# Copying the queries of a batch's first group in two halves, in a cross attention kernel on one Trainium2 core

## The chip, the core and the metric

The kernel runs on one core of a Trainium2 chip. The metric is the device time of one execution in microseconds (us), as the median of some runs. Matrix products run on TensorE (PE in the profile; its weight loads are a row of their own, PEld). Elementwise work runs on VectorE (DVE), ScalarE (ACT) and GpSimd (POOL). SyncE (SP) issues most of the DMA transfers. The engines run side by side and hand work over by semaphores: an instruction raises one when it is finished, and another engine's instruction waits until it has reached a value.

## The reference, cut to what matters

`x` is 32 batches of 512 tokens of width 640, and `ctx` is 32 batches of 77 text tokens of width 1024. There are 20 heads of width 32. The reference also has three other attention branches (object, others, ip), whose contexts are empty slices here, so that only the text branch counts:

```python
q = _heads(hidden_states @ to_q_w)                 # 32 x 20 x 512 x 32
k, v = _heads(ehs_txt @ to_k_w), _heads(ehs_txt @ to_v_w)   # 32 x 20 x 77 x 32
s = jnp.einsum('bhqd,bhkd->bhqk', q, k) * scale
p = jax.nn.softmax(s, axis=-1)
out = _merge(jnp.einsum('bhqk,bhkd->bhqd', p, v))
out = out @ to_out_w + to_out_b + hidden_states
```

## The kernel before, in words

There are two phases. `project_context` splits the weights into a high and a low part and computes keys and values of all batches into DRAM; it takes about the first 316 us. `attend` does the rest, and the change is there alone.

`attend` goes through 32 batches, and in each through 5 groups of 4 heads (`CC = 5` groups of 128 columns, `QT = 4` tiles of 128 queries). Every engine has an order written out by hand, one string for each group (lines 66 to 81), and all engines run their strings independently, held together by semaphores alone. A letter is an operation of that group's step:

- TensorE: `S` are the scores of this group (`scores`, L755: 4 tiles x 4 heads, 16 calls and 32 matmul instructions). `Q0` to `Q4` project the queries of the *next* group into the PSUM bank `q_bank` (`project_q`, L743, 15 matmuls). `P` and `O` are output projections of earlier batches (15 matmuls each), and `V` is the product of the probabilities with the values, two groups back (`sum_values`, L770, 8 instructions).
- VectorE: `M` is the maximum over the keys (`maxima`, L636), `R0` to `R3` the reciprocals of the sums of a tile, `T0` to `T3` the transposes of its probabilities, `Q` the copy of `q_bank` to `q_t` in SBUF (`copy_q`, L657, one instruction of 512 columns), `W` a correction of the head outputs, `X` and `Y` prepare x of the next batch, and `O`, `P`, `Z` finish outputs.
- ScalarE: `S0` to `S3` are the exponentials of the four tiles (`exps`), `V` a copy of the head outputs. GpSimd: `N0` to `N3` multiply the probabilities with the reciprocals.

The strings of a batch's last group are what the change touches:

```
TensorE  g=4:  S O2 Q0 Q1 Q2 Q3 Q4 V      then g=0 of the next batch:  S Q0 ...
VectorE  g=4:  M X2 X3 X4 W R0 R1 T0 O2 R2 T1 Q R3 T2 T3    then:  M W Z0 ...
VectorE  g=0:  M W Z0 R0 Q R1 T0 Z1 R2 T1 R3 T2 Z2 T3 P3
```

In the groups 0 to 3 TensorE has an output projection between the last `Q` and the next `S` (but for the start of the run); in group 4 it has only `V`. The scores wait for the keys of the batch (only in group 0), for the exponentials of the group before (`exp_done`, they free the PSUM bank) and for the copy of the queries (`q_ready`), then raise `scores_clear`, for which no engine waits. The profile shows waits that don't fit into an instruction as EVENT_SEMAPHORE instructions of TensorE's sequencer: one at L761 in each group, and a further one at L760 in the first group of a batch, where there are three waits.

Of the kernel before, what the change touches and what calls it, by code (L numbers as in the profile page):

```python
# [28 lines left out]
CC = C // P  # L29
KC = CA // P  # L30
QT = S // P
# [59 lines left out]
def cross_attention(nc, x, ctx, wq, wk, wv, wo, bias, out):  # L91
    k_scratch = nc.dram_tensor("k_scratch", (C, TOK), F32, kind="Internal").ap()
    v_scratch = nc.dram_tensor("v_scratch", (TOK, C), F32, kind="Internal").ap()
    p_scratch = nc.dram_tensor("p_scratch", (2, KB, P, HG * P), F32, kind="Internal").ap()
    with ExitStack() as stack:
        def sbuf(name, shape, dtype=F32):
            return stack.enter_context(nc.sbuf_tensor(name, shape, dtype))


        kept = {  # L100
            "x_raw": sbuf("x_raw", [P, 2, S // SQ, CQ]),
            "wq": sbuf("wq_split", [P, 2, CC, C], F32R),
            "wo": sbuf("wo_split", [P, 2, CC, C], F32R),
        }
        x_loaded = stack.enter_context(nc.semaphore("x_loaded"))
        x_v = x.rearrange("b (n q) (i c) -> b i q n c", q=SQ, i=P // SQ)
        out_v = out.rearrange("b (n q) (i c) -> b i q n c", q=SQ, i=P // SQ)
        project_context(nc, ctx, wq, wk, wv, wo, kept, k_scratch, v_scratch, x_v, x_loaded)
        attend(nc, x_v, bias, out_v, kept, k_scratch, v_scratch, p_scratch, x_loaded)
# [305 lines left out]
def attend(nc, x_v, bias, out_v, kept, k_scratch, v_scratch, p_scratch, x_loaded):  # L415

    with ExitStack() as stack:
        def sbuf(name, shape, dtype=F32):
            return stack.enter_context(nc.sbuf_tensor(name, shape, dtype))

        def sem(name):
            return stack.enter_context(nc.semaphore(name))
# [8 lines left out]
        q_t = [sbuf(f"q_t{i}", [P, S]) for i in range(2)]  # L431
# [12 lines left out]
        q_bank, pv_bank, fill_bank = bank[0], bank[1], bank[2:4]  # L444
# [4 lines left out]
        scores_clear, s_done, max_ready, exp_done = sem("scores_clear"), sem("s_done"), sem("max_ready"), sem("exp_done")  # L449
# [1 line left out]
        probs_zero, probs_turned, pv_done = sem("probs_zero"), sem("probs_turned"), sem("pv_done")  # L451
        probs_written = [sem(f"probs_written{i}") for i in range(2)]
        probs_read = [sem(f"probs_read{i}") for i in range(2)]
        q_done, q_ready = sem("q_done"), sem("q_ready")
        ot_high, ot_ready = sem("ot_high"), sem("ot_ready")
        xt_turned, xt_high, xt_ready = sem("xt_turned"), sem("xt_high"), sem("xt_ready")
        out_done, out_added, out_turned, out_stored = (sem("out_done"), sem("out_added"), sem("out_turned"),
# [6 lines left out]
        def tiles_of(columns):  # L464

            return columns.rearrange("p (t i q) -> p t i q", t=QT, q=SQ)

        def rows_of(columns):

            return columns.rearrange("p (i t q) -> p t i q", t=QT, q=SQ)  # L470
# [164 lines left out]
        def _(dve):  # L635
# [21 lines left out]
            def copy_q(n, slot):  # L657
                dve.wait_ge(q_done, n + 1)
                if not (isinstance(n, int) and n < 2):
                    dve.wait_ge(s_done, n - 1)  # L660
                nc.vector.tensor_copy(tiles_of(q_t[slot][:, :]), rows_of(q_bank[:, :])).then_inc(q_ready, 1)  # L661

            def ot_low_part(b, g, parity):
                dve.wait_ge(ot_high, CC * b + g + 1)
# [33 lines left out]
            for c in range(CC):  # L698
                xt_low_part(0, c)
            copy_q(0, 0)  # L700

            def body(b, parity, age, last):
# [37 lines left out]
        def _(pe):  # L740
# [14 lines left out]
            def scores(b, g, slot, parity):  # L755
                if g == 0:
                    pe.wait_ge(k_loaded[parity], DMA // 2 * (b - parity) + DMA)
                if not (isinstance(b, int) and CC * b + g == 0):
                    pe.wait_ge(exp_done, TILES * b + QT * g)
                pe.wait_ge(q_ready, CC * b + g + 1)  # L760
                pe.sem_inc(scores_clear, 1)  # L761
                for t in range(QT):
                    for h in range(HG):
                        rows = slice(h * HD, (h + 1) * HD)
                        last = nc.tensor.matmul(s_bank[:, h, t * N_TXT:(t + 1) * N_TXT],  # L765
                                                q_t[slot][rows, t * P:(t + 1) * P], k_sb[parity][rows, g, :],
                                                start=True, stop=True)
                last.then_inc(s_done, 1)
# [28 lines left out]
            def body(b, parity, age, last):  # L797
                for g, slot, kind, k in steps(TENSOR, b, parity, age, last):
                    if kind == "S":
                        scores(b, g, slot, parity)  # L800
                    elif kind == "Q":
                        project_q(*after(b, g), k)
                    elif kind == "V":
                        sum_values(*before(b, g, parity, 2)[:2], slot)
                    elif kind == "O":
                        project_out(b - 1, k, 1 - parity)
                    elif kind == "P":
                        project_out(b - 2, k, parity)
# [28 lines left out]
```

## Time and profile before

| | |
|---|---|
| time, median of 3 runs | 1820.34 us (1820.07 to 1821.33) |
| the profiled execution: its own time | 1821.04 us |
| its span, first to last instruction | 1819.2 us |
| mean granted TensorE clock | 0.987 |
| PE busy | 1756.4 us, 97% |
| PEld busy | 1364.8 us, 75% |
| DVE busy | 1282.9 us, 71% |
| ACT busy | 1052.6 us, 58% |
| POOL busy | 496.5 us, 27% |

A busy PE is a matmul in flight; matmuls overlap, and their ends are modelled. A row of the timeline is a run of instructions of one line: start, length, engine, line, operation, what is written from what, shapes, count, and in brackets the idle time of the engine before it with what ended it.

### The profile page before, as it was taken

How to read it: one execution, taken by the hardware profiler on the slowest of the kernel's cores; microseconds unless marked ns; L12 is line 12 of the kernel's file. 1: busy time of each engine (PE TensorE's matmuls, PEld its weight loads, DVE VectorE, ACT ScalarE, POOL GpSimd, SP SyncE). 2: the span in 40 equal slices, each digit the busy share in tenths (PEclk: the TensorE clock that was granted, in tenths of full speed). 3: DMA queues.
4: the chain of work that ended last, by engine and by line, in shares of the span. 5: the costliest groups of instructions: out<-in, count | busy, mean ns of one | idle time of the engine just before them, and what ended most of it. 6: DMA issues, size and time to landing. Idle time of an engine off the chain costs nothing.

```text
span 1819.2 us, 38127 instructions
## 1 busy us (share of the span) xinstructions
PE 1756.4 (97%) x13360; PEld 1364.8 (75%) x13360; DVE 1282.9 (71%) x2506; ACT 1052.6 (58%) x5597; POOL 496.5 (27%) x735
## 2 busy tenths in 40 slices
PE   7999996799999999999999999999999999999996
PEld 7999995567777777777777777777777777777764
DVE  5321201678888888888888888888888888888873
ACT  4321211666666666666666666666666666666660
POOL 1111110333333333333333333333333333333330
PEclk9999998899999999999999999999999999999998
DMA  9543112587888888888888888888888888888863
GB/s 229 152 121 92 63 47 58 142 204 214 224 220 223 222 222 224 226 219 221 225 227 219 223 223 223 230 215 222 223 224 229 217 224 223 223 224 224 220 185 103
DMA packets 311599, 357.00 MB, mean 196 GB/s; under 512 B 40240, under 2 KB 194592, under 8 KB 311408
## 3 DMA queue, kind: packets, MB, share of 16 engines
q1 hardware_dynamic: 241648, 301.30, 61.0%
q10 hardware_dynamic: 65472, 40.64, 10.4%
q0 software_dynamic: 4288, 12.62, 2.0%
q8 instruction: 106, 1.74, 0.4%
q14 instruction: 85, 0.70, 0.1%
HBM read 174.10 MB, written 180.39 MB: 195 GB/s over the span
## 4 chain that ended last, share of the span: by engine, by line
PE 78%; DVE 2%; ACT 1%; DMA 1%; issue 1%; POOL 0%; SPq 0%; ACTq 0%; DVEq 0%
PE p_bank L750 31%; PE p_bank L789 29%; PE p_scores L765 9%; PE p_bank L777 8%; ACT probs L597 1%; DVE negmax L638 0%; DMA p_scratch<-turned 0%; DMA out<-out_blocks 0%; DVE turned L654 0%; POOL probs L574 0%; DMA probs_t<-p_scratch 0%; DVE x_t L676 0%; DVE x_raw L671 0%; DVE out_blocks L692 0%; SPq L518 0%
## 5 line engine op out<-in xcount | busy, mean ns | idle before, releaser
L597 ACT ACTIVATE probs<-p_scores,negmax 128x77 f32<-128x77 f32 x2560 | 788.7, 361 | 325.9 <-DVE negmax L638 325.9
L574 POOL TENSOR_TENSOR probs<-probs,rsum 128x308 f32<-128x308 f32 x640 | 447.4, 701 | 1021.1 <-DVE rsum L644 1021.0
L597 ACT ACTIVATION_READ_ACCUMULATOR probs<-p_scores,negmax 128x1 f32 x2560 | 619.5, 242 | 0.0
L750 PE MATMUL p_bank<-x_t,wq_split 128*128 128x512 f32 x2400 | 596.4, 401 | 16.0 <-DVE x_t L676 16.0
L789 PE MATMUL p_bank<-o_t,wo_split 128*128 128x512 f32 x2400 | 574.9, 391 | 0.4 <-DVE x_turned L685 0.4
L750 PEld LDWEIGHTS p_bank<-x_t,wq_split 128*128 128x128 f32 x2400 | 446.8, 190 | 116.3 <-DVE x_t L676 17.2
L789 PEld LDWEIGHTS p_bank<-o_t,wo_split 128*128 128x128 f32 x2400 | 448.7, 188 | 98.0 <-issue 2.5
L654 DVE STREAM_TRANSPOSE turned<-probs 128x384 f32<-128x384 f32 x640 | 352.4, 551 | 39.9 <-POOL probs L574 39.8
L765 PEld LDWEIGHTS p_scores<-k_sb,q_t 32*128 32x128 f32 x5120 | 159.8, 187 | 152.8 <-issue 152.8
L638 DVE TENSOR_REDUCE negmax<-p_scores 128x16 f32<-128x1232 f32 x160 | 230.2, 1438 | 24.0 <-PE p_scores L765 23.8
L604 ACT ACTIVATE o_t<-p_bank 128x512 fp32r<-128x512 f32 x160 | 98.5, 616 | 177.3 <-PE p_bank L777 177.3
L765 PE MATMUL p_scores<-k_sb,q_t 32*128 32x77 f32 x5120 | 182.5, 279 | 18.6 <-ACT probs L597 11.6
L644 DVE RECIPROCAL rsum<-sums 128x4 f32<-128x4 f32 x640 | 107.5, 168 | 125.7 <-ACT probs L597 121.2
L777 PE MATMUL p_bank<-probs_t,v_sb 77*32 77x512 f32 x1280 | 171.3, 607 | 8.6 <-DMA probs_t<-p_scratch 6.3
L661 DVE COPY q_t<-p_bank 128x512 f32<-128x512 f32 x160 | 109.4, 684 | 81.4 <-PE p_bank L750 81.4
L377 PE MATMUL p_bank<-ctx_t,wk_split 128*128 128x256 f32 (+1 forms) x1200 | 147.2, 285 | 9.9 <-DVE wk_split L315 9.6
L377 PEld LDWEIGHTS p_bank<-ctx_t,wk_split 128*128 128x128 f32 x1200 | 146.2, 195 | 10.2 <-DVE wk_split L315 9.6
L397 PE MATMUL p_bank<-wv_split,ctx_t 128*128 128x320 f32 (+1 forms) x960 | 142.2, 309 | 0.0
L397 PEld LDWEIGHTS p_bank<-wv_split,ctx_t 128*128 128x128 f32 (+1 forms) x960 | 139.0, 184 | 1.7
L333 DVE TENSOR_TENSOR ctx_t<-ctx_turned,ctx_t 128x512 fp32r<-128x512 f32 (+1 forms) x40 | 26.7, 668 | 149.1 <-ACT ctx_t L264 148.9
L665 DVE TENSOR_TENSOR o_t<-p_bank,o_t 128x512 fp32r<-128x512 f32 x160 | 108.8, 680 | 0.0
L280 ACT ACTIVATE kv_out<-p_bank 128x320 f32<-128x320 f32 (+1 forms) x40 | 17.5, 437 | 113.0 <-PE p_bank L397 108.0
(30 smaller groups left out, 706.7 us busy)
## 6 DMA issues: line engine op xcount, KB each, us to landing
p_scratch<-turned SPq DMA_DIRECT2D x160, 768.0 KB, 5.9
probs_t<-p_scratch SPq DMA_DIRECT2D x320, 256.0 KB
out<-out_blocks SPq DMA_DIRECT2D x128, 320.0 KB, 5.5
x_raw<-in_x ACTq DMA_DIRECT2D x124, 320.0 KB, 4.4
probs_t<-p_scratch SPq DMA_DIRECT2D x160, 104.0 KB
ctx_raw<-in_ctx SPq DMA_DIRECT2D x32, 256.0 KB, 8.6
k_sb<-k_scratch SPq DMA_DIRECT2D x32, 192.5 KB, 5.1
v_sb<-v_scratch SPq DMA_DIRECT2D x160, 38.5 KB
```

Source lines behind the costliest of these rows:

```text
L377: last = nc.tensor.matmul(bank[n % BANKS][:, 0:tokens], wk_s[:, a, k, m * P:(m + 1) * P], ctx_t[j % 2][:, b, k, 0:tokens], start=k == 0 an ...
L397: last = nc.tensor.matmul(bank[n % BANKS][0:rows, 0:HALF], ctx_t[j % 2][:, a, k, t0:t0 + rows], wv_s[:, b, k, hf * HALF:(hf + 1) * HALF], ...
L574: nc.gpsimd.tensor_tensor(heads_of(t), heads_of(t), rsum[:, slot, t, :].unsqueeze(2).to_broadcast([P, HG, N_TXT]), ALU.mult).then_inc(prob ...
L597: last = nc.scalar.activation(heads_of(t)[:, h, :], s_bank[:, h, t * N_TXT:(t + 1) * N_TXT], ACT.Exp, bias=negmax[:, slot, t, h:h + 1], ac ...
L638: nc.vector.tensor_reduce(negmax[:, slot, :, :], s_bank[:, :, 0:QT * N_TXT].rearrange("p h (t k) -> p t h k", k=N_TXT), AX.X, ALU.max, neg ...
L654: nc.vector.transpose(turned[slot][:, :, :, t, :].rearrange("p k h q -> p h k q"), squares_of(t)).then_inc(probs_turned, 1)
L661: nc.vector.tensor_copy(tiles_of(q_t[slot][:, :]), rows_of(q_bank[:, :])).then_inc(q_ready, 1)
L665: nc.vector.tensor_tensor(o_t[parity][:, 1, g, :], pv_bank[:, :], o_t[parity][:, 0, g, :].bitcast(F32), ALU.subtract).then_inc(ot_ready, 1)
L750: last = nc.tensor.matmul(q_bank[:, :], wq_s[:, w, c, g * P:(g + 1) * P], x_t[:, a, c, :], start=c == 0 and i == 0, stop=c == CC - 1 and i ...
L765: last = nc.tensor.matmul(s_bank[:, h, t * N_TXT:(t + 1) * N_TXT], q_t[slot][rows, t * P:(t + 1) * P], k_sb[parity][rows, g, :], start=Tru ...
L777: last = nc.tensor.matmul(pv_bank[h * HD:(h + 1) * HD, :], v_sb[:, g, h * HD:(h + 1) * HD], probs_t[slot][:, :, h, :], start=True, stop=True)
L789: last = nc.tensor.matmul(fill_bank[n % 2][:, :], wo_s[:, w, c, k * P:(k + 1) * P], o_t[parity][:, o, c, :], start=c == 0 and i == 0, stop ...
```

## The change

The copy of the queries of a group 0 (all batches but the first) is made as two instructions of 256 columns each (two query tiles). The first raises a new semaphore `q_half`, the second raises `q_ready`. The scores of such a group wait for `q_half` ahead of their first tile, and for `q_ready` (and raise `scores_clear` again) ahead of their third. All other groups are as before.

```diff
-        q_done, q_ready = sem("q_done"), sem("q_ready")
+        q_done, q_ready, q_half = sem("q_done"), sem("q_ready"), sem("q_half")
...
                 dve.wait_ge(q_done, n + 1)
                 if not (isinstance(n, int) and n < 2):
                     dve.wait_ge(s_done, n - 1)
-                nc.vector.tensor_copy(tiles_of(q_t[slot][:, :]), rows_of(q_bank[:, :])).then_inc(q_ready, 1)
+                halves = [slice(0, QT // 2), slice(QT // 2, QT)] if n % CC == 0 and n > 0 else [slice(0, QT)]
+                for part in halves:
+                    nc.vector.tensor_copy(tiles_of(q_t[slot][:, :])[:, part], rows_of(q_bank[:, :])[:, part])\
+                      .then_inc(q_ready if part is halves[-1] else q_half, 1)
...
                     pe.wait_ge(exp_done, TILES * b + QT * g)
-                pe.wait_ge(q_ready, CC * b + g + 1)
+                in_halves = g == 0 and b > 0
+                if in_halves:
+                    pe.wait_ge(q_half, b)
+                else:
+                    pe.wait_ge(q_ready, CC * b + g + 1)
                 pe.sem_inc(scores_clear, 1)
                 for t in range(QT):
+                    if in_halves and t == QT // 2:
+                        pe.wait_ge(q_ready, CC * b + 1)
+                        pe.sem_inc(scores_clear, 1)
                     for h in range(HG):
```

## Rows read from the trace of the kernel before

**Rows 1.** The page: busy time by engine, and the chain that ended last.

```profile
PE 1756.4 (97%) x13360; PEld 1364.8 (75%) x13360; DVE 1282.9 (71%) x2506; ACT 1052.6 (58%) x5597; POOL 496.5 (27%) x735
...
PE 78%; DVE 2%; ACT 1%; DMA 1%; issue 1%; POOL 0%; SPq 0%; ACTq 0%; DVEq 0%
```

**Rows 2.** Timeline of PE from 999 us, steps 4 and 0 to 2 of two batches.

```profile
999.47 1.07 PE L777 MATMUL p_bank<-probs_t,v_sb 77*32 77x512 f32 x8
1000.68 1.13 PE L765 MATMUL p_scores<-k_sb,q_t 32*128 32x77 f32 x32
...
1008.77 1.07 PE L777 MATMUL p_bank<-probs_t,v_sb 77*32 77x512 f32 x8
1009.76 1.13 PE L765 MATMUL p_scores<-k_sb,q_t 32*128 32x77 f32 x32
...
1018.84 1.13 PE L765 MATMUL p_scores<-k_sb,q_t 32*128 32x77 f32 x32
```

**Rows 3.** Timeline of PE, the first groups of batches 2 and 31.

```profile
407.46 1.13 PE L765 MATMUL p_scores<-k_sb,q_t 32*128 32x77 f32 x32
...
1730.57 1.13 PE L765 MATMUL p_scores<-k_sb,q_t 32*128 32x77 f32 x32
```

**Rows 4.** PEld: the scores' weight loads of 407 to 1775 us grouped, and one second group.

```profile
L765 PEld LDWEIGHTS p_scores<-k_sb,q_t 32*128 32x128 f32 x4800 | 148.3, 186 | 131.7 <-issue 131.7
...
1009.76 0.98 PEld L765 LDWEIGHTS p_scores<-k_sb,q_t 32*128 32x128 f32 x32 [0.84 <-issue]
```

**Rows 5.** Timeline of DVE around the copy, and the maxima one group later.

```profile
999.77 0.65 DVE L661 COPY q_t<-p_bank 128x512 f32<-128x512 f32 x1
1000.35 0.16 DVE L644 RECIPROCAL rsum<-sums 128x4 f32<-128x4 f32 x1
...
1001.32 0.58 DVE L654 STREAM_TRANSPOSE turned<-probs 128x384 f32<-128x384 f32 x1 [0.35 <-POOL probs L574]
1001.87 1.44 DVE L638 TENSOR_REDUCE negmax<-p_scores 128x16 f32<-128x1232 f32 x1
...
1010.96 1.44 DVE L638 TENSOR_REDUCE negmax<-p_scores 128x16 f32<-128x1232 f32 x1 [0.23 <-PE p_scores L765]
```

**Rows 6.** All copies (line 661): ns min/median/max, first and last start.

```profile
L661 DVE COPY q_t<-p_bank x160: 649/692/692, 316.4 to 1762.6; 128x512 f32<-128x512 f32 x160
```

**Rows 7.** DVE groups by shape: one operation at 512 and at 320 columns.

```profile
L327 DVE STREAM_TRANSPOSE ctx_turned<-ctx_raw 128x512 f32<-128x512 f32 x36 | 25.2, 704 | 22.2 <-DMA ctx_raw<-in_ctx 22.1
...
L327 DVE STREAM_TRANSPOSE ctx_turned<-ctx_raw 128x320 f32<-128x320 f32 x4 | 2.0, 505 | 0.0
```

**Rows 8.** Waits of TensorE's sequencer (lines 760, 748), and PE after the latter.

```profile
L760 PEldq EVENT_SEMAPHORE  x31: 51/51/51, 362.4 to 1730.4; - x31
...
L748 PEldq EVENT_SEMAPHORE  x1: 51/51/51, 1038.1 to 1038.1; - x1
...
1038.06 3.69 PE L789 MATMUL p_bank<-o_t,wo_split 128*128 128x512 f32 x15
1041.60 3.56 PE L750 MATMUL p_bank<-x_t,wq_split 128*128 128x512 f32 x15
```

**Rows 9.** All matmuls of the scores (line 765), ns min/median/max.

```profile
L765 PE MATMUL p_scores<-k_sb,q_t x5120: 270/270/492, 317.2 to 1767.8; 32*128 32x77 f32 x197
```

**Rows 10.** Timeline of ACT: the last exponential of the first group.

```profile
1008.08 0.29 ACT L597 ACTIVATION_READ_ACCUMULATOR probs<-p_scores,negmax 128x1 f32 x1
```

**Rows 11.** Batch 1's groups 0 and 1 on PE, and the late one of batch 6.

```profile
362.57 1.13 PE L765 MATMUL p_scores<-k_sb,q_t 32*128 32x77 f32 x32 [0.68 <-DVE q_t L661]
...
370.40 1.13 PE L765 MATMUL p_scores<-k_sb,q_t 32*128 32x77 f32 x32 [2.08 <-ACT probs L597]
...
590.08 1.01 PEld L765 LDWEIGHTS p_scores<-k_sb,q_t 32*128 32x128 f32 x32 [1.18 <-issue]
```

**Rows 12.** Two stretches: busy us of the engines (count), clock, DMA share, GB/s.

```profile
400.00:1775.00 1375.00, 1367.98 (x10521) 1007.10 (x10519) 1134.66 (x2254) 920.00 (x5128) 421.76 (x604) 1.00 0.83 221
...
1776.00:1782.00 6.00, 3.56 (x12) 1.64 (x13) 2.56 (x5) 0.60 (x1) 0.00 (x0) 0.50 0.66 206
```

## The prediction

> **What bounds the kernel now.** I read the page first. PE is busy for 97% of the span, and the chain that ended last runs on PE for 78% of it, with 1% of "issue" [rows 1]; DVE has 2% of the chain. So this is a TensorE kernel, and a change can help only where PE's own row has a hole. The timeline of PE shows one hole for each batch. In an undisturbed group the scores' first matmul starts 0.99 us after the first of the values product: 1008.77 to 1009.76. In the first group of a batch it is 1.21 us: 999.47 to 1000.68 [rows 2]. Everything else repeats: one group takes 9.08 us (1009.76 to 1018.84), so five take 45.40. Batches 2 to 31 stand 1730.57 - 407.46 = 1323.11 us apart at their first groups, which is 29 periods of 45.62 [rows 3]. The difference of 0.22 us is the hole and nothing else. A grouped row agrees: the weight loads of 150 steps (4800 instructions, 32 each) sat idle for 131.7 us; 120 steps at 0.84 us are 100.8, and the other 30 have 1.03 us each, 0.19 more [rows 4].
>
> What ends the hole is the copy of the queries: it starts at 999.77 and ends at 1000.42, and the matmul follows at 1000.68, 0.26 us later [rows 5, 2]. Without it the matmul could start at 999.47 + 0.99 = 1000.46. The copy starts late not because TensorE is late but because VectorE is still at other work: no idle time stands before it. In batch 1 the profile names the copy as releaser (0.68 us) [rows 11]; in the others it says "issue", since the wait sits in the sequencer instruction at L760, which is there 31 times, once for each batch from 1 on [rows 8].
>
> **The change part by part.** *First half of the copy.* The long copy takes 0.65 us (the minimum; the median of 0.692 belongs to the groups where VectorE had been idle) [rows 6]. No row shows 256 columns. The slope comes from one VectorE operation at two widths: (704 - 505) / 192 = 1.04 ns for a column [rows 7], so 650 - 256 x 1.04 = 0.38 us. Bounds: half of 0.65 (0.325, no fixed part at all) and 0.505, a 320-column operation. I take 0.39, near the slope's value. It ends at 1000.16; with the same 0.26 us the scores could start at 1000.42, which is 0.04 before TensorE is ready for them. With the upper bound they would start at 1000.54, and 0.14 of the 0.22 us would still be won. So the gain at the head is 0.14 to 0.22, and I take 0.22.
>
> *Second half.* The copy and the reciprocal behind it start 0.58 us apart at 0.65 us of length, so 0.07 overlaps [rows 5]. The second half starts at 999.77 + 0.32 = 1000.09 and ends at 1000.48. The third tile's matmuls are due half of the scores' stream (1.06 us from the first score matmul to the next projection) after 1000.46, at 1000.99. Even with 0.26 us for the wait they are released at 1000.74. So the second wait is met long before its turn.
>
> *The added wait in the middle, 31 times.* A met wait costs the sequencer an instruction, 0.05 us recorded [rows 8]. What is queued behind it are the second 16 score matmuls, then the next projection, and with the scores the maxima. Whether TensorE feels it depends on how far the sequencer is ahead. The trace shows a wait of this kind within a stream: that of L748, taken at 1038.1, while the 15 matmuls in front of it have only begun at 1038.06; the projection behind it starts at 1041.60, 3.54 later, without a hole [rows 8]. So 15 weight loads and 15 matmuls can lie ahead. In the scores the lead is smaller, since their instructions are short: bounds 0 and 0.26 us (the whole price that the wait at the head has, exposed). I take 0.01, near the row in the stream.
>
> *VectorE's extra instruction.* It adds 0.38 - 0.07 + 0.32 - 0.58, about 0.05 us, in front of R3, T2, T3 and the next M; the bounds are 0 and 0.13 (a second full 0.20 less the overlap). R3 releases GpSimd, which releases T3, which is followed by M without idle time at 1001.87 [rows 5]. So M does not come earlier when the scores do: against TensorE it is 0.22 + 0.05 = 0.27 us later than now. Who waits? The exponentials, and with them the scores of group 1. The last exponential ends at 1008.37 [rows 10], the scores of group 1 start at 1009.76 [rows 2]. This is a cover of 1.39 us less 0.26 for the wait; 0.27 goes into it. The maxima of group 1 have 0.23 us of idle time before them [rows 5], and so do those of groups 2 and 3, so the lateness is used up within the batch and is not carried to its next copy. If that cover were gone, each 0.1 us would cost 3 us.
>
> A rule of the Trainium skill speaks against the edit: the page "VectorE: DVE Perf Modes", section "The TRN2 errata", says that the fixed cost comes once for each instruction, some 150 cycles, so that many small tiles pay it many times, and it advises tiles of 512 elements or more. For the copies here the trace has 0.65 us at 512 columns. By the page the second instruction would put 0.16 us on VectorE instead of 0.05, M would be 0.38 late instead of 0.27, and the sum would be the same by both, as the cover holds either.
>
> *Batch 1* has the same hole (0.68 us), but its group 1 waits for the exponentials at 370.40, 2.08 us idle [rows 11]. They hang on M, and M on T3. So what the scores win is lost there; I count 0.05 us lost. *Batch 6* has a start at 590.08 with 1.18 us idle instead of 1.03 [rows 11]; a second sequencer delay of 0.15 us lies behind the copy, and as the sequencer is free 0.26 us earlier I leave the usual 0.22 of gain. *The end* (the last values product waits for DMA) moves with the rest, and so does a stretch at half clock, granted 0.50 from 1776 to 1782 against 1.00 from 400 to 1775 [rows 12]. It falls behind an idle time of PE that the change leaves alone; where it falls against the work can shift by some tenths, which I estimate at 1 us either way from the 1.3 us between the three runs.
>
> **Sum.** Batches 2 to 31 are 30 first groups: 30 x 0.22 = 6.6. Less 31 x 0.01 for the wait, less 0.05 for batch 1: 6.2 us. The profiled execution took 1821.04 us, its span 1819.2; it would be 1814.8. It lies 0.7 above the median, so the median would be 1820.34 - 6.2 = 1814.1.
>
> **The rivals.**
> *A: the middle wait is partly exposed.* For it: the sequencer starts this stream with an empty lead, for it has just stood at the head, and the two waits there cost time too. Against: the wait in the stream without a hole [rows 8], and that the first half's 16 calls are issued in front of it. At 0.10 us for each batch 3.1 us are lost: 1817.1.
> *B: nothing is won.* The middle wait costs its full 0.26 us, or the whole of what the head wins: between 1819.5 and 1821.5, I say 1820.4. The same time results if the first half raises its semaphore only when the second is done. For it only that no row shows two such instructions in a row; against it that R3 starts and releases GpSimd right behind the copy.
> *C: slower.* The wait in the middle drains the array: the second half's first weight load goes out only after the last matmul of the first half has ended (0.27 us [rows 9]) and then the 0.26 us of the wait follow, 0.53 us in all. Less 0.22 that is 0.31 us for each batch, 31 x 0.31 = 9.6: 1829.9. Its place is the scores' third tile, and it decides from the point where the middle wait costs more than 0.22 us. For it: the head shows 0.26 us between a semaphore and the matmul. Against it: the second half has been ready for 0.25 us when its turn comes, so nothing need be waited for there.
> *D: the lateness of M reaches the scores of group 1.* It would take 1.1 us where 0.27 to 0.4 are to be had: not above 1 in 100, and I fold it into C.
> The Trainium skill's page "TensorE: Matmul & The Clock Gate" gives the queue a depth of 64. By this the half stream of 32 instructions fits in ahead of the wait, as in the forecast; the trace shows 30 instructions ahead.
>
> **How the numbers follow.** Forecast 0.76, with an own range of 1813.0 to 1815.6 (all head gains at 0.22 and no middle cost, 1813.8, less 0.8 for the end; middle cost 0.05, 1815.4). A 0.12, B 0.06, C with D 0.06. The range takes in the forecast and the larger part of A: 1812.8 to 1817.6; outside are B, C and a small rest. What a measurement of this kernel tells from no change is about 0.2%, 3.6 us: faster is below 1816.7. That is the forecast and half of A (0.82), same is the other half of A and most of B (0.12), slower is C (0.06).
>
> **What the profile after would show.** PE's timeline: from the values product to the scores 0.99 us in first groups, as in the others; 1.21 would refute the head's gain. The scores' stream 1.06 us to the next projection; more is the middle wait's cost (A: 1.16, C: 1.6). First groups 45.40 to 45.42 us apart. Copies of 256 columns at 0.38 to 0.40 us, 31 of each half. M of the first group 0.3 us behind the end of the scores, that of group 2 at the old distance. The sequencer's wait for the second half taken before the third tile. The prediction is wrong if the periods of the batches stay above 45.5, or if they shrink and the time does not: then something at the start or the end took it.

## The result

| | time, median us | runs | time of the profiled execution | its span |
|---|---|---|---|---|
| before | 1820.95 (1820.07 to 1824.09) | 6 | 1821.04 | 1819.2 |
| after | 1812.62 (1810.99 to 1813.86) | 6 | 1813.24 | 1811.4 |

The ratio is 0.995, with a 95% interval of 0.9937 to 0.9962, so the kernel is faster, by 0.4 to 0.6%. Against a forecast of 1814.1 and a range of 1812.8 to 1817.6 the median lies 0.2 us below the range. The profiled executions differ by 7.8 us, and the forecast worked out 6.2. So the direction and the place were right and the size was too small. Two later comparisons of the same two kernels gave 1813.31 against 1819.76 (0.9966, 0.9952 to 0.9979) and 1812.28 against 1820.29 (0.9959, 0.9945 to 0.9972).

The page of the kernel after: busy times, and the chain that ended last. Against [rows 1], the share of "issue" is gone and DVE is 4 us busier.

```profile
PE 1753.9 (97%) x13360; PEld 1363.8 (75%) x13360; DVE 1287.0 (71%) x2537; ACT 1052.0 (58%) x5597; POOL 495.5 (27%) x735
...
PE 78%; DVE 2%; ACT 1%; DMA 1%; POOL 0%; issue 0%; SPq 0%; ACTq 0%; DVEq 0%
```

The timeline of PE after, the first group of a batch and the values product behind it; L787 is the values product, L775 the scores, L753 the query projection, L799 the output projection:

```profile
996.13 1.06 PE L787 MATMUL p_bank<-probs_t,v_sb 77*32 77x512 f32 x8
997.13 1.13 PE L775 MATMUL p_scores<-k_sb,q_t 32*128 32x77 f32 x32
998.19 3.69 PE L753 MATMUL p_bank<-x_t,wq_split 128*128 128x512 f32 x15
...
1005.21 1.06 PE L787 MATMUL p_bank<-probs_t,v_sb 77*32 77x512 f32 x8
1006.21 1.02 PE L775 MATMUL p_scores<-k_sb,q_t 32*128 32x77 f32 x28
```

The first group's scores now start 1.00 us after the values product (996.13 to 997.13), as in the next group, where [rows 2] had 1.21 and 0.99. The projection follows the scores after 1.06 us, as it did before: the wait in the middle costs TensorE nothing.

The first groups of batches 2 and 31:

```profile
406.93 1.13 PE L775 MATMUL p_scores<-k_sb,q_t 32*128 32x77 f32 x32
...
1723.53 1.13 PE L775 MATMUL p_scores<-k_sb,q_t 32*128 32x77 f32 x32
```

They are 1316.60 us apart, which is 29 periods of 45.40, exactly five groups of 9.08; [rows 3] had 45.62. The grouped weight loads of the scores from 407 to 1775 us lost 5.9 us of idle time against [rows 4]:

```profile
L775 PEld LDWEIGHTS p_scores<-k_sb,q_t 32*128 32x128 f32 x4800 | 147.4, 186 | 125.8 <-issue 125.8
```

VectorE around the copy and at the next group's maxima, then its copies by shape, and the added waits of the sequencer:

```profile
996.43 0.72 DVE L663 COPY q_t<-p_bank 128x256 f32<-128x256 f32 x2
997.08 0.16 DVE L644 RECIPROCAL rsum<-sums 128x4 f32<-128x4 f32 x1
...
998.55 1.40 DVE L638 TENSOR_REDUCE negmax<-p_scores 128x16 f32<-128x1232 f32 x1
...
1007.41 1.44 DVE L638 TENSOR_REDUCE negmax<-p_scores 128x16 f32<-128x1232 f32 x1
```

```profile
L663 DVE COPY q_t<-p_bank 128x256 f32<-128x256 f32 x62 | 22.2, 397 | 0.0
```

```profile
L772 PEldq EVENT_SEMAPHORE  x31: 51/51/51, 362.2 to 1723.6; - x31
L772 PEldq EVENT_SEMAPHORE  x1: 51/51/51, 997.2 to 997.2; - x1
```

The two halves take 0.72 us together where the whole took 0.65, and the reciprocal starts 0.65 after the copy instead of 0.58 [rows 5]: 0.07 us for the extra instruction. The middle wait (L772; the second row is the one of this batch) is taken at 997.19, 0.04 us after the second half's end at 997.15. In all 31 batches it is 0.04 to 0.08 us, and the least is also what r6 shows for a wait that is too late. So in this kernel TensorE's sequencer most likely stands at the middle wait until the second half is there, and costs nothing by it, because the weight loads of the third tile begin only at 997.57, 0.38 us later. The maxima of the first group start 1.42 us after the scores (997.13 to 998.55) where they started 1.19 after [rows 2, 5], so they are 0.23 later against TensorE. The maxima of the second group have lost the idle time that [rows 5] shows before them, but start at the old distance from the scores, 1.20 us (1006.21 to 1007.41). The lateness ends there, as worked out.

### The profile page after: what moved, and what is told of

It is laid out like the page before. It is cut to its first block, busy times and chain, and to the rows that moved or that the text cites. A ratio compares the mean times of both kernels' runs of the same rounds, so it can differ in the third digit from the quotient of the medians.

```text
span 1811.4 us, 38189 instructions
## 1 busy us (share of the span) xinstructions
PE 1753.9 (97%) x13360; PEld 1363.8 (75%) x13360; DVE 1287.0 (71%) x2537; ACT 1052.0 (58%) x5597; POOL 495.5 (27%) x735
## 3 DMA queue, kind: packets, MB, share of 16 engines
q10 hardware_dynamic: 65472, 40.64, 10.2%
## 4 chain that ended last, share of the span: by engine, by line
PE 78%; DVE 2%; ACT 1%; DMA 1%; POOL 0%; issue 0%; SPq 0%; ACTq 0%; DVEq 0%
PE p_bank L753 31%; PE p_bank L799 30%; PE p_scores L775 9%; PE p_bank L787 8%; ACT probs L597 1%; DVE negmax L638 0%; DMA out<-out_blocks 0%; DMA p_scratch<-turned 0%; DVE turned L654 0%; POOL probs L574 0%; DMA probs_t<-p_scratch 0%; DVE x_t L679 0%; DVE x_raw L674 0%; DVE out_blocks L695 0%; SPq L518 0%
## 5 line engine op out<-in xcount | busy, mean ns | idle before, releaser
L597 ACT ACTIVATION_READ_ACCUMULATOR probs<-p_scores,negmax 128x1 f32 x2560 | 627.0, 245 | 0.0
L753 PE MATMUL p_bank<-x_t,wq_split 128*128 128x512 f32 x2400 | 595.7, 400 | 15.7 <-DVE x_t L679 15.6
L799 PE MATMUL p_bank<-o_t,wo_split 128*128 128x512 f32 x2400 | 575.2, 392 | 0.4 <-DVE x_turned L688 0.4
L753 PEld LDWEIGHTS p_bank<-x_t,wq_split 128*128 128x128 f32 x2400 | 446.3, 190 | 115.8 <-DVE x_t L679 16.9
L799 PEld LDWEIGHTS p_bank<-o_t,wo_split 128*128 128x128 f32 x2400 | 449.0, 188 | 97.8 <-issue 2.5
L775 PEld LDWEIGHTS p_scores<-k_sb,q_t 32*128 32x128 f32 x5120 | 159.1, 188 | 146.7 <-issue 146.7
L775 PE MATMUL p_scores<-k_sb,q_t 32*128 32x77 f32 x5120 | 182.7, 279 | 13.6 <-ACT probs L597 12.8
L787 PE MATMUL p_bank<-probs_t,v_sb 77*32 77x512 f32 x1280 | 171.3, 607 | 8.0 <-DMA probs_t<-p_scratch 5.8
L663 DVE COPY q_t<-p_bank 128x512 f32<-128x512 f32 (+1 forms) x191 | 111.5, 596 | 75.0 <-PE p_bank L753 75.0
```

Of the source, the lines that this page charges most:

```text
L597: last = nc.scalar.activation(heads_of(t)[:, h, :], s_bank[:, h, t * N_TXT:(t + 1) * N_TXT], ACT.Exp, bias=negmax[:, slot, t, h:h + 1], ac ...
L663: nc.vector.tensor_copy(tiles_of(q_t[slot][:, :])[:, part], rows_of(q_bank[:, :])[:, part])\
L753: last = nc.tensor.matmul(q_bank[:, :], wq_s[:, w, c, g * P:(g + 1) * P], x_t[:, a, c, :], start=c == 0 and i == 0, stop=c == CC - 1 and i ...
L787: last = nc.tensor.matmul(pv_bank[h * HD:(h + 1) * HD, :], v_sb[:, g, h * HD:(h + 1) * HD], probs_t[slot][:, :, h, :], start=True, stop=True)
L799: last = nc.tensor.matmul(fill_bank[n % 2][:, :], wo_s[:, w, c, k * P:(k + 1) * P], o_t[parity][:, o, c, :], start=c == 0 and i == 0, stop ...
```

## The experiments

Of each profile I took three things: the steady part (first group of batch 2 to first group of batch 31), the end (from there to the end of the span), and the step from the values product to the scores in a first group. All in us; the ratio is to the kernel before, in the same comparison.

| kernel | values to scores | steady part | end | ratio (95%) |
|---|---|---|---|---|
| before | 1.21 | 1323.1 | 88.6 | |
| after | 1.00 | 1316.6 | 87.9 | 0.9950 (0.9937 to 0.9962) |
| r1 after again | 1.00 | 1316.6 | 87.5 | 0.9966 (0.9952 to 0.9979) |
| r2 before again | 1.20 | 1322.9 | 88.6 | 1.0003 (0.9994 to 1.0012) |
| r3 copy earlier | 1.06 | 1318.6 | 92.2 | 0.9984 (0.9975 to 0.9992) |
| r4 halves on VectorE alone | 1.27 | 1324.6 | 92.3 | 1.0017 (1.0008 to 1.0026) |
| r5 three met waits | 1.24 | 1324.5 | 92.2 | 1.0014 (1.0003 to 1.0025) |
| r6 second half late | 1.00 | 1326.7 | 87.9 | 1.0011 (0.9999 to 1.0022) |
| r7 three and one tile | 1.11 | 1319.7 | 88.1 | 0.9967 (0.9956 to 0.9979) |
| r8 batch 1 as before | 1.00 | 1316.6 | 87.6 | 0.9955 (0.9940 to 0.9970) |
| r9 after, third time | 1.00 | 1316.7 | 87.8 | 0.9959 (0.9945 to 0.9972) |
| r10 earlier and halves | 1.00 | 1316.6 | 87.5 | 0.9958 (0.9946 to 0.9970) |
| r11 halves in last 8 | both | 1321.4 | 89.6 | 1.0002 (0.9992 to 1.0012) |
| r12 halves in last 15 | both | 1319.8 | 88.1 | 0.9973 (0.9963 to 0.9983) |
| r13 halves in last 22 | both | 1318.3 | 86.6 | 0.9981 (0.9973 to 0.9990) |

**r1, r9 and r2: both kernels again.** No edit.

> The changed kernel as it stands, timed again. What is open is why it gained 7.8 us in its profile and about 8.3 in the medians where 6.2 was forecast. Theory N (the steady part is all that the change does; the rest is chance at the start and the end): the first groups of batches 2 and 31 are again 29 periods of 45.40 us apart, that is 6.5 to 6.8 us less than before, while the stretch ahead of batch 2 and the one behind batch 31 differ from the first profile by several tenths either way; the gain in the medians is 6.5 to 7.5 us. Theory S (something systematic outside the steady part, 1 to 1.5 us at start and end): both stretches show the same shortening again (0.3 ahead of batch 2, 0.7 behind batch 31), and the medians differ by 7.8 us or more.

> The kernel before against itself: a null. Theory N: its profile has the steady part unchanged to 0.1 us (29 periods of 45.62), while the time ahead of batch 2 and behind batch 31 differs from the first profile by 0.3 us and up to 1 us, since a DMA landing and a stretch at half clock lie there. Theory S: both stretches agree with the first profile to 0.1 us, and the excess belongs to the change. Ratio 1.000 by both, with an interval that says what this kernel's measurement can tell.

> The changed kernel a third time, since the first comparison gave 8.3 us and the second 6.2. What stands open is only the size. Theory N: steady part 29 periods of 45.40 to 0.05 us; start of batch 2 anywhere from 405 to 408 us and the stretch behind batch 31's first group 87.5 to 88.7 us, or some 92 where a second stretch at half clock falls into it, as in the profiles of four other kernels; median gain 6.0 to 7.5 us. Theory S: 7.8 to 8.5 us again.

The steady part repeats to 0.14 us in the changed kernel and to 0.23 us in the one before; the difference is 6.1 to 6.5 us in every pairing. The start of batch 2 does not repeat: 407.46 and 405.21 us in the two profiles of the kernel before, 406.93, 405.23 and 405.78 in those of the changed one. So the 0.5 us by which the first pair of profiles differed there is not the change's. The end does repeat, and there theory N did not fare well: 88.6 twice before, 87.9, 87.5 and 87.8 after. Nor did theory S get its 7.8 us each time: the medians differ by 8.3, 6.5 and 8.0. The null comparison gives 1.0003 (0.9994 to 1.0012).

**r3: the copy one transpose earlier, whole.**

```diff
-                "M X2 X3 X4 W R0 R1 T0 O2 R2 T1 Q R3 T2 T3")
+                "M X2 X3 X4 W R0 R1 T0 O2 R2 Q T1 R3 T2 T3")
```

> No halves, no added wait: the kernel before with the copy put one transpose earlier in VectorE's last group (Q T1 in place of T1 Q). If the hole is only the copy's lateness on VectorE (my theory), the copy waits for the projection's end (about 0.13 us after the values product began) and ends at +0.79; with 0.26 the scores start at about 1.05 us after the values product in place of 1.21: 0.16 us for each batch, 5 us in all. Rival: the transposes and reciprocals that are pushed back by 0.5 us reach the scores of the second group (their cover is 1.1 us), and the gain is less than 3 us.

PE and DVE of r3 in a first group:

```profile
997.44 1.06 PE L777 MATMUL p_bank<-probs_t,v_sb 77*32 77x512 f32 x8
998.50 1.13 PE L765 MATMUL p_scores<-k_sb,q_t 32*128 32x77 f32 x32
```

```profile
997.55 0.69 DVE L661 COPY q_t<-p_bank 128x512 f32<-128x512 f32 x1 [0.20 <-PE p_bank L750]
```

Now the copy waits for TensorE (0.20 us idle before it) and no longer for VectorE. The step to the scores is 1.06 us and the steady part 4.5 us shorter, 0.16 for each batch. So the start of the scores follows the copy; the 0.06 us that are left fall away once the first half is enough (r10). The ratio says 1.5 to 4.6 us less, and the medians differ by 3.1. The profiled execution, whose end took 92.2 us, took the longest of the eleven (1820.07 against a median of 1816.67), so its end is not that of the typical execution. The profiled executions of r4 (1825.49 against 1823.12) and r5 (1826.34 against 1824.26) lie above their medians too.

**r4: halves, but one wait for both.** The scores' lines are those of the kernel before.

> The copy in two halves, but the scores wait once, for both: what the extra VectorE instruction costs when nobody uses the first half. By my theory the second half ends 0.06 us later than the whole copy did, so the scores of the 31 first groups start 0.06 us later: values product to scores 1.27 us, period 45.68, and 1.5 to 2 us more in time. Rival (some of the gain comes from VectorE's side and not from the earlier start): not slower than before, or faster.

```profile
999.29 1.06 PE L780 MATMUL p_bank<-probs_t,v_sb 77*32 77x512 f32 x8
1000.55 1.13 PE L768 MATMUL p_scores<-k_sb,q_t 32*128 32x77 f32 x32 [0.20 <-DVE q_t L663]
```

The step is 1.26 to 1.27 us (the second row names the copy as releaser), the steady part 1.5 us longer, the time 1.5 to 4.7 us longer. The extra instruction costs 0.05 us where it stands in front of TensorE, and the gain comes from using the first half alone.

**r5: three met waits in every group's scores**, 480 in all, one ahead of each of the tiles 1 to 3, with the whole copy.

```diff
                 for t in range(QT):
+                    if t > 0:
+                        pe.wait_ge(q_ready, CC * b + g + 1)
+                        pe.sem_inc(scores_clear, 1)
```

> The kernel before, whole copy, but with a wait for the queries (met) and a raise of scores_clear ahead of the second, third and fourth tile of the scores in all 160 groups: 480 waits of the kind of which the change adds 31. Theory (a met wait within the stream is hidden by the sequencer's lead): the scores' stream stays at 1.06 us to the next matmul, period 45.62, time within noise of before. Rival A of the prediction (each costs 0.05 to 0.1 us): the stream takes 1.2 to 1.36 us, the period 46.4 to 47.1, time 24 to 48 us more. Between the two: the first wait is hidden and later ones are not, since the lead shrinks by about 0.1 us for each.

The waits are there, and the scores' stream keeps its length: 1.07 us from 1001.53 to 1002.60, and 1.06 in most batches.

```profile
L765 PEldq EVENT_SEMAPHORE  x480: 51/51/51, 317.6 to 1768.8; - x160
```

```profile
1000.30 1.06 PE L780 MATMUL p_bank<-probs_t,v_sb 77*32 77x512 f32 x8
1001.53 1.13 PE L768 MATMUL p_scores<-k_sb,q_t 32*128 32x77 f32 x32 [0.17 <-issue]
1002.60 3.74 PE L750 MATMUL p_bank<-x_t,wq_split 128*128 128x512 f32 x15
```

The steady part is 1.4 us longer for 435 such waits within it, 0.05 us for a batch of 15. Most of it shows in the values-to-scores step of the first groups: 1.23 or 1.24 us where before had 1.21 or 1.22, and 1.32 to 1.34 in seven of the thirty. Why it shows there is open, as the added waits stand behind the start of these scores. The groups 1 to 3 of a batch take 9.08 us with and without the waits. Rival A had 24 to 48 us here; it is refuted. My 0.01 us for one wait is refuted by the change itself: its period of 45.40 leaves nothing for the wait in the middle.

**r6: the second half behind T2**, so that the middle wait is not yet met.

```diff
-                "M X2 X3 X4 W R0 R1 T0 O2 R2 T1 Q R3 T2 T3")
+                "M X2 X3 X4 W R0 R1 T0 O2 R2 T1 Q R3 T2 H T3")
...
+                    elif kind == "H":
+                        copy_q(CC * b + g + 1, 1 - slot, "second")
```

> The changed kernel with the second half of the copy moved behind the transpose T2 on VectorE in the last group, so that it ends at about 1.55 us after the values product began, just after the third tile's turn at 1.53: the wait in the middle is no longer met. What an unmet wait costs. If only the lateness counts (ready at 1.55, plus the 0.26 us seen at the head): the third tile starts at about 1.81 in place of 1.53, 0.28 us for each batch, period 45.68, some 8 us slower than the change. Rival C of the prediction (the array drains and refills besides): 0.5 us or more, period 45.9, 15 us.

The weight loads of one first group, and the second half's copy:

```profile
1003.40 0.54 PEld L778 LDWEIGHTS p_scores<-k_sb,q_t 32*128 32x128 f32 x16 [0.84 <-issue]
1004.16 0.56 PEld L778 LDWEIGHTS p_scores<-k_sb,q_t 32*128 32x128 f32 x16 [0.22 <-issue]
```

```profile
1003.65 0.39 DVE L664 COPY q_t<-p_bank 128x256 f32<-128x256 f32 x1
```

Here the middle wait is seen: the loads come in two runs of 16. The second run starts 0.12 us after the copy's end (1004.04). The stream is 0.34 us longer (1003.40 to 1004.80, 1.40 in place of 1.06) and the steady part 10.1 us longer than the change's, 0.35 for each batch where 0.28 was expected. Both parts of my estimate were off: the half ends 1.63 us after the values product and not 1.55, and the wait behind it takes 0.12 and not 0.26, so the loads come at 1.75. As 0.34 is what they are late, their turn had been at 1.41, ahead of the matmuls' 1.53; in the changed kernel they begin at 1.44 (997.57 less 996.13). Rival C (0.5 us or more) is more than even an unmet wait costs, and this is what the change would be with its halves too far apart.

**r7: three tiles and one.**

```diff
-                halves = [slice(0, QT // 2), slice(QT // 2, QT)] if n % CC == 0 and n > 0 else [slice(0, QT)]
+                halves = [slice(0, QT - 1), slice(QT - 1, QT)] if n % CC == 0 and n > 0 else [slice(0, QT)]
```

> The changed kernel with the copy split 3 to 1 (384 and 128 columns) and the middle wait ahead of the fourth tile. The first part takes 0.39 + 0.13 = 0.52 us and ends 0.83 us after the values product began; with 0.26 the scores start at 1.09, where TensorE is ready at 0.99 to 1.00. So 0.13 of the 0.22 us are won: values product to scores about 1.09 us, period 45.49, some 2.7 us slower than the change. Rival (the start of the scores is bound by something else than the copy's end plus 0.26): the period stays at 45.40.

```profile
L663 DVE COPY q_t<-p_bank 128x384 f32<-128x384 f32 x31 | 16.1, 521 | 0.0
L663 DVE COPY q_t<-p_bank 128x128 f32<-128x128 f32 x31 | 8.6, 276 | 0.0
```

0.52 us for 384 columns as worked out, a step of 1.11 and a period of 45.51. The start of the scores follows the first part's end until TensorE itself is the later, which is between 256 and 384 columns.

**r8: batch 1 as before** (`n > CC` and `b > 1` in the two conditions).

> The changed kernel, but batch 1 keeps its whole copy and its one wait; the halves begin with batch 2. Tells what batch 1 brings. My term: it loses 0.05 us. The profiles so far (407.46 to 406.93 for the start of batch 2, but 405.21 in a second profile of the kernel before) can't tell. In this profile: batch 1's scores start 1.7 us after the values product (before: 1.74, changed 1.26 to 1.4), and the second group of batch 1 starts 7.83 us after the first as before, where the changed kernel has about 8.02; the two together are worth 0.1 to 0.2 us if the exponentials' wait gives part of the gain back, 0 if all of it. Steady part 45.40 as in the change.

Groups 0 and 1 of batch 1, in r8 and in the changed kernel:

```profile
361.36 1.13 PE L775 MATMUL p_scores<-k_sb,q_t 32*128 32x77 f32 x32 [0.85 <-DVE q_t L663]
...
369.20 1.13 PE L775 MATMUL p_scores<-k_sb,q_t 32*128 32x77 f32 x32 [2.10 <-ACT probs L597]
```

```profile
362.09 1.13 PE L775 MATMUL p_scores<-k_sb,q_t 32*128 32x77 f32 x32 [0.53 <-ACT probs L597]
...
370.11 1.13 PE L775 MATMUL p_scores<-k_sb,q_t 32*128 32x77 f32 x32 [2.27 <-ACT probs L597]
```

The two groups are 7.84 us apart in r8 and 8.02 in the changed kernel. The second waits for ScalarE in both, so what batch 1's scores win is handed back there. From the values product to the second group it is 9.57 us before and 9.62 after in the first pair of profiles, the 0.05 us lost that the sum had. But r2 (before) has 9.90, and the changed kernel has 9.84 in r1 and 9.56 in r9, r8 itself 9.76: the start's scatter covers a term of this size, so it is not shown.

**r10: both, the earlier copy and the halves.**

> The changed kernel with the copy also one transpose earlier on VectorE (Q T1 in place of T1 Q). The hole was closed already with about 0.04 to 0.07 us to spare, so theory: the period stays at 45.40 and the time within noise of the changed kernel; the copy starts 0.17 us earlier, and the maxima of the first group are about 0.5 us behind the scores in place of 0.28. Rival: there is still something of the copy in the head, and the period falls below 45.40.

Steady part and step as in the changed kernel, time the same (1812.28 for both in one comparison). The hole is closed, and nothing is left in it. The maxima of the first group are 0.6 us behind the scores' end here, and those of the second group start 1.38 us after the scores instead of 1.20, so the lateness ends one group later than in the change.

**r11, r12 and r13: the halves in the last 8, 15 and 22 batches alone**, to move the place where the steady part ends without touching anything else.

```diff
-                halves = [slice(0, QT // 2), slice(QT // 2, QT)] if n % CC == 0 and n > 0 else [slice(0, QT)]
+                halves = [slice(0, QT // 2), slice(QT // 2, QT)] if n % CC == 0 and n >= 24 * CC else [slice(0, QT)]
```

> The changed kernel with the halves (and the middle wait) in the last 8 batches alone. It tells what the excess at the end is. The stretch from batch 31's first group to the end of the span was 87.5 to 87.9 us in five profiles whose steady part (first group of batch 2 to first group of batch 31) is 1316.6 to 1316.7, 88.6 in both profiles of the kernel before (1323.1, 1322.9), 88.1 at 1319.7, 87.9 at 1326.7, but 92.2 in all three kernels at 1318.6, 1324.5 and 1324.6, where PE ran a second stretch at half clock after its short idle time. Theory P (the end's length depends on where the steady part ends against the steps at which the granted clock changes, and so an edit that shortens the steady part changes the end as well): here the steady part is 1323.1 - 8 x 0.225 = 1321.3, which lies from 1324.5 by as much as 1318.6 from 1321.9, in the bad region: the end takes 92 us, and the kernel is 1.5 to 2 us SLOWER than before though its steady part is 1.8 us shorter. Theory N (the end is chance): end 87.5 to 88.7 more often than not, kernel 1.8 us faster than before.

> The same with the last 15 batches: steady part 1323.1 - 3.4 = 1319.7, where another kernel had an end of 88.1 us. Theory P: end 88 us, the whole 3.4 to 4 us arrives in the time. Theory N: 3.4 us faster as well, with an end that is as likely as before to be 92. The two kernels together: theory P has the 15 batches 5 to 6 us faster than the 8 batches, theory N 1.6 us.

> The halves in the last 22 batches. Steady part 1323.1 - 22 x 0.225 = 1318.1 to 1318.2, close to the 1318.6 at which another kernel had an end of 92.2 us. Theory P (the end's length follows from where the steady part ends): the end takes about 92 us in the profile, 4 more than at 15 batches, and of the 4.95 us that the steady part gains only 1 to 3 arrive: median 1817.5 to 1819 against 1820.3, slower than or equal to the kernel with 15 batches although 7 more holes are closed. Theory N (the end is chance): 1.6 us faster than with 15 batches, 5 us faster than before.

The steady parts came out as worked out (1321.4, 1319.8, 1318.3). The times did not follow them:

| | steady part shorter by | time shorter by, from the ratio (interval) |
|---|---|---|
| last 8 | 1.7 | -0.4 (-2.2 to 1.5) |
| last 15 | 3.3 | 4.9 (3.1 to 6.7) |
| last 22 | 4.8 | 3.5 (1.8 to 4.9) |
| all 31 (three comparisons) | 6.5 | 9.1, 6.2, 7.5 |

From 8 to 15 batches, in one comparison, the median falls by 5.4 us where seven holes are worth 1.6: theory P had 5 to 6, theory N 1.6. From 15 to 22 another seven holes bring nothing that the intervals can tell, and the medians say 1817.44 against 1815.30; P had this too. But the granted clock is in this step too: five of the eleven executions with 8 batches have a mean granted clock of 0.985 or 0.986 and take 1821.5 to 1823.6 us, and none of the nine with 15 has. Without the five the medians are 3.7 us apart. P's word on the profiles was wrong twice: an end of 92 us was expected at 8 and 22 batches, and the two profiles had 89.6 and 86.6. The twelve times of the kernel with 22 batches fall in two heaps, 1811.4 to 1814.7 (five) and 1817.2 to 1819.5 (seven). The mean granted clock on record separates them: 0.988 or 0.989 in the five, 0.986 or 0.987 in the seven. So the same kernel can go either way from one execution to the next. That the length of the steady part sets how often is not shown: in the kernel before the share of executions at 0.985 or 0.986 was 3 of 27, 9 of 26, 2 of 9, 4 of 19 and 0 of 17 in the five later comparisons.

What the ends consist of can be read in the timeline of PE behind the last group. First before and after:

```profile
1778.43 1.93 PE L777 MATMUL p_bank<-probs_t,v_sb 77*32 77x512 f32 x8 [5.79 <-DMA probs_t<-p_scratch]
1780.30 4.86 PE L789 MATMUL p_bank<-o_t,wo_split 128*128 128x512 f32 x15
1787.37 1.07 PE L777 MATMUL p_bank<-probs_t,v_sb 77*32 77x512 f32 x8 [2.21 <-DVE o_t L665]
1788.37 13.94 PE L789 MATMUL p_bank<-o_t,wo_split 128*128 128x512 f32 x60
```

```profile
1770.41 1.94 PE L787 MATMUL p_bank<-probs_t,v_sb 77*32 77x512 f32 x8 [4.82 <-DMA probs_t<-p_scratch]
1772.28 5.20 PE L799 MATMUL p_bank<-o_t,wo_split 128*128 128x512 f32 x15
1779.69 1.07 PE L787 MATMUL p_bank<-probs_t,v_sb 77*32 77x512 f32 x8 [2.21 <-DVE o_t L668]
1780.69 13.89 PE L799 MATMUL p_bank<-o_t,wo_split 128*128 128x512 f32 x60
```

And r4, whose end is 92.3, with its busy times and clock in two stretches:

```profile
1781.00 5.66 PE L792 MATMUL p_bank<-o_t,wo_split 128*128 128x512 f32 x15
1788.87 1.93 PE L780 MATMUL p_bank<-probs_t,v_sb 77*32 77x512 f32 x8 [2.21 <-DVE o_t L668]
1790.73 16.10 PE L792 MATMUL p_bank<-o_t,wo_split 128*128 128x512 f32 x60
```

```profile
1778.50:1785.00 6.50, 5.87 (x17) 3.38 (x18) 0.94 (x2) 0.60 (x1) 0.00 (x0) 0.50 0.71 192
1789.00:1795.00 6.00, 6.00 (x18) 3.47 (x18) 0.00 (x0) 0.60 (x1) 0.00 (x0) 0.50 0.00 0
```

Two things vary. The first is the transfer for the batch's second last values product, which TensorE waits for: 5.79 us idle before, 4.82 after, which is 1.0 us. SyncE's rows of this transfer, before and after, say which part of it: L522 issues the write of the probabilities, and L530 issues the reads once it has landed.

```profile
1767.14 0.38 SPq L522 DMA_DIRECT2D p_scratch<-turned  x1
1773.26 1.24 SPq L530 DMA_DIRECT2D probs_t<-p_scratch  x3
...
1760.09 0.38 SPq L522 DMA_DIRECT2D p_scratch<-turned  x1
1765.21 1.24 SPq L530 DMA_DIRECT2D probs_t<-p_scratch  x3
```

The write is issued 36.57 and 36.56 us after the first scores of batch 31, and the product starts 5.2 us behind the reads in both. Between the two lie 6.12 us before and 5.12 after: the write lands 1.0 us sooner. In r2, the second profile of the kernel before, it takes 6.1 us, in r1, r8, r9 and r10 4.4 to 4.8. It does not follow the length of the steady part: r6, with the longest (1326.7), has 4.0, and r11 (1321.4) has 6.5. TensorE sits idle for 6.46 us in r11 and for 4.92 in r12, which is nearly the whole difference of their ends (89.6 and 88.1 us).

The second is the granted clock. Within that idle time or just behind it, it falls to half (0.50, that is 1.2 GHz) in all kernels, in most of them for 6.8 us; at half clock the eight matmuls of a values product take 1.93 us instead of 1.07. In r3, r4 and r5 it is at half a second time, behind TensorE's second idle time of 2.21 us, and the output projections take 16.1 us in place of 13.9. In r13, whose end is the shortest, the stretch at half clock is over after 3.4 us:

```profile
1773.00:1776.20 3.20, 3.20 (x13) 1.69 (x6) 1.26 (x3) 0.60 (x1) 0.00 (x0) 0.50 0.60 223
1776.40:1783.00 6.60, 4.39 (x23) 2.68 (x22) 2.04 (x3) 0.60 (x1) 0.00 (x0) 1.00 0.43 96
```

In the first pair of profiles the stretch at half clock is there once in both, 6.8 us long. So the 0.75 us of the change's gain that lie at the end are the transfer's 0.97 less what the projection at half clock gave back (5.20 against 4.86), and 0.1 us in what follows.

## Why the prediction was right in its place and too small in its size

- *The hole and its cause.* Right. Its size, 0.22 us, was right, the period went to 45.40, and r3 and r7 move the start of the scores with the copy's end as worked out.
- *First half 0.39 us, ready ahead of TensorE.* Right: a minimum of 0.383, and all of the 0.22 us was won. (Two slips of the prediction's working change nothing in it: in front of the middle wait stand 8 calls with 16 matmuls, not 16 calls, and rival A comes to 1816.9 by its own terms, not 1817.1.)
- *The middle wait, 0.01 us for each batch.* Too high. It costs TensorE nothing here (a period of 45.40, five groups of 9.08), which is 0.3 us of the sum. That the second half is there ahead of the third tile's turn was right; that the wait is already met when the sequencer reaches it most likely was not, and what hides it is the 0.38 us until the third tile's loads. Both rivals that rested on it, A and C, are refuted, by the change's own 1.06 us and by r5; r6, whose second half ends 0.6 us later, pays 0.35. B is refuted by the step of 1.00 us.
- *VectorE's extra instruction, 0.05 us.* 0.07 in the profile after and 0.05 in r4, hidden behind the maxima's cover as said. The Trainium skill ("VectorE: DVE Perf Modes", section "The TRN2 errata") measured the 150 cycles behind the prediction's 0.16 us on a copy from SBUF to SBUF; its row for a source in PSUM, as here, has 120 cycles, which makes an estimate of 0.13 us. The trace has less than either, 0.07, since the second half starts before the first has ended. By the page as by the row the time is the same.
- *Batch 6's second sequencer delay kept at the usual gain.* Too low. In the changed kernel the delay is gone there, as the periods of batches 2 to 31 are all 45.40; with rounding (0.225 for 0.22) this is 0.1 us.
- *The end moves with the rest, 1 us either way.* This is the step that failed: it counted 0 and measured 0.75 us in the first pair, and about 1.0 between the two ends of before (88.6) and the five of kernels whose steady part is 1316.6 or 1316.7 (87.5 to 87.9, three of them the changed kernel's). What did not move with the rest is the wait for the transfer: 5.79 us of idle time before (5.78 in r2), and 4.82, 4.39 and 4.56 in the three profiles of the changed kernel, as the write of the probabilities lands sooner. The prediction looked for its scatter in the half-clock stretch, which is the same in both and gave 0.34 us of this back. The stretch can differ elsewhere (twice in r3 to r5, 3.4 us in r13). With the middle wait at 0 and the end at 0.75 the forecast would have been 1813.0, 0.4 us from the median.
- *The range.* The forecast's own lower end was 1813.0, without the middle wait's 0.3 us, with 0.8 for the end and nothing for the start; the stated one is 0.2 below it. The start came out 0.4 us from the forecast in the first pair, and it differed by 2.3 us between two profiles of one kernel. With a scatter of this size a lower bound 1.3 us under the forecast was too near. That the median fell outside by 0.2 us is in part luck: of the changed kernel's three medians, 1812.62, 1813.31 and 1812.28, the second lies within the range.
- *The 8.3 us between the medians.* Part of this is luck as well, as two of the six executions before took 1824.0 and 1824.1. In the five later comparisons 18 of 98 executions of the kernel before have a mean granted clock of 0.985 or 0.986, with times of 1822.1 to 1827.0, and none of the 27 executions of the changed kernel, r8 and r10 has. Without the 18 the medians differ by 6.2 us for r1 and 7.4 for r9. Whether the change keeps the kernel out of these executions is not shown.

The first pair's profiles add up as: 0.53 us up to batch 2 (forecast 0.15), 6.51 in the steady part (6.09) and 0.75 at the end (0), 7.8 in all.

What stays open: why the write ahead of the end lands 1 us sooner, and what decides how long and how often the clock is at half in an end, and with it between the two heaps of r13. Both were only read from profiles, not forced by an experiment.

## What to carry to other kernels

A consumer on the critical engine that waits for a copy can start on its first half, if the engine's own readiness lies between the two halves' ends; look how much the first part may hold before its end is the later (here between 256 and 384 columns), and keep the second part ahead of its turn, as a second half 0.6 us later cost more than the hole did (0.35 against 0.22 us). Price a repeated saving by the period of the loop in the profile, which repeated to 0.01 us for a batch here while the times of one kernel in one comparison scattered by 2 to 9 us, and price the stretches outside the loop separately. If those hold a wait and a change of clock, they can differ by as much as a small edit gains.

## What the runs showed of the hardware that was not expected

- Three more waits in each scores' stream cost 1.4 us for the 435 of the steady part, none of it in the groups 1 to 3 of a batch (r5).
- The wait in the middle, released 0.04 us after the second half's end, cost nothing with 0.38 us left until the loads behind it (the change).
- From the end of a copy to the first weight load behind it, it took 0.12 us with one wait instruction in between (r6) and 0.23 us with two (before: 1000.42 to 1000.65).
- The end took 86.6 to 92.3 us for the same work, with the granted clock at half once or, in r3, r4 and r5, twice, for 3.4 to 10.2 us at a time, and with a write that took 4.0 to 6.5 us until the reads behind it were issued. Closing 22 holes instead of 15 brought no measurable time (r12, r13).
- The two heaps of r13's times differ in the mean granted clock: 0.988 or 0.989 against 0.986 or 0.987.
